# Queries stored once and split head by head, and two turning steps moved in their pipelines

## The reference

```python
h = layernorm(x) * (1 + ca) + sa
x = x + ga * attn(h, Wq, Wk, Wv, Wo)       # 16 heads, 4 key/value heads of 64, rotary, ALiBi, softmax over 1024 keys
h = layernorm(x) * (1 + cb) + sb
x = x + gb * ffn(h, ...)                   # two layers of local attention and gated MLP
...
# in attn
q = (x @ Wq).reshape(b, l, H, HD); k, v with KV = 4 heads, repeated 4 times
attn = softmax(rope(q) @ rope(k).T / sqrt(HD) + slopes * rel)
# in each of the 2 layers of ffn: 8 heads of 64, window 64 (this window and the one before it)
q, k = l2norm(q) * qs, l2norm(k) * ksc, both rotated and scaled by position
x = x + softmax(8 * q @ k.T + mask) @ v @ wo
x = x + (a * gelu(g)) @ w2 + b2
```

## Time and profile before

| | |
|---|---|
| median of 3 runs | 1131.87 us (1130.56 to 1132.34) |
| profiled execution, own time | 1133.57 us |
| its span, first to last instruction | 1131.8 us |
| TensorE busy | 1062.1 us (94%) |
| VectorE busy | 833.3 us (74%) |
| GpSimd busy | 747.3 us (66%) |
| ScalarE busy | 670.9 us (59%) |
| first matmul of the global attention | at 107.50 us |

### The profile page before, as it was taken

How to read it: one execution, slowest core, us unless ns; L and a number is a source line. 1 busy time by engine, 2 the same in 40 slices (tenths; PEclk the granted TensorE clock), 3 DMA queues, 4 the chain that set the end, 5 groups by cost and what they waited for, 6 DMA issues and landing times. The chain is left out here.

```text
span 1131.8 us, 23099 instructions
## 1 busy us (share of the span) xinstructions
PE 1062.1 (94%) x8304; PEld 654.9 (58%) x8304; DVE 833.3 (74%) x1522; ACT 670.9 (59%) x1222; POOL 747.3 (66%) x510
## 2 busy tenths in 40 slices
PE   6884799999999999999999999889999797999988
PEld 3552455555555555555555554766677694776778
DVE  6995666666666666666666674589999689999857
ACT  2552366566665665666666655047887556887744
POOL 3662466767686767776676768679986238756526
PEclk9996799999999999999999999999999999999989
DMA  8899622524315124242152100101111100111101
GB/s 255 276 275 357 161 57 48 112 53 93 80 50 122 40 66 104 67 92 69 48 113 71 44 20 21 38 10 32 33 43 34 25 2 19 33 34 33 44 17 36
DMA packets 82624, 88.48 MB, mean 78 GB/s; under 512 B 32036, under 2 KB 65360, under 8 KB 82512
## 3 DMA queue, kind: packets, MB, share of 16 engines
q1 hardware_dynamic: 82512, 87.01, 29.9%
HBM read 53.04 MB, written 24.24 MB: 68 GB/s over the span
## 5 line engine op out<-in xcount | busy, mean ns | idle before, releaser
L871 DVE CUSTOM_DVE_ANT_0 junk<-psum,alibi 128x1024 bf16<-128x1024 f32 x256 | 313.2, 1223 | 200.7 <-PE psum L942 191.8
L843 ACT ACTIVATE E<-psum,keybias_sb 128x1024 f32<-128x1024 f32 x256 | 274.7, 1112 | 229.6 <-PE psum L966 216.3
L774 POOL TENSOR_TENSOR sum_p<-sum_p,E 128x1024 f32<-128x1024 f32 x96 | 232.4, 2421 | 90.4 <-ACT E L843 85.8
L978 PE MATMUL psum<-E,V 128*64 128x512 f32 x1024 | 248.1, 605 | 0.0
L942 PE MATMUL psum<-KH,QH 64*128 64x512 f32 x512 | 118.7, 459 | 12.9 <-PEq L274 7.4
L978 PEld LDWEIGHTS psum<-E,V 128*64 128x64 f32 x1024 | 62.2, 136 | 112.3 <-issue 98.4
L780 POOL TENSOR_TENSOR sum_p<-sum_p,xpos_sb 128x1024 f32<-128x1024 f32 x32 | 76.3, 2384 | 69.0 <-DVE xpos_sb L881 69.0
L942 PEld LDWEIGHTS psum<-KH,QH 64*128 64x128 f32 x512 | 49.5, 189 | 121.9 <-DVE M L871 84.5
L966 PE MATMUL psum<-QH,KH 64*128 64x512 f32 x512 | 102.2, 395 | 2.1 <-DVE M L871 2.1
L966 PE MATMUL psum<-QL,KH 64*128 64x512 f32 x512 | 101.6, 392 | 0.0
L966 PE MATMUL psum<-QH,KL 64*128 64x512 f32 x512 | 101.5, 392 | 0.0
(11 more groups left out here) (149 smaller groups left out, 2008.3 us busy)
## 6 DMA issues: line engine op xcount, KB each, us to landing
QH<-qa_scratch SPq DMA_DIRECT2D x64, 256.0 KB, 4.2
qa_scratch<-tH SPq DMA_DIRECT2D x8, 1024.0 KB, 5.4
qa_scratch<-tL SPq DMA_DIRECT2D x8, 1024.0 KB, 7.9
QL<-qa_scratch SPq DMA_DIRECT2D x64, 128.0 KB, 4.2
vp_att<-v_att SPq DMA_DIRECT2D x64, 128.0 KB, 2.3
XF<-inverse_scratch SPq DMA_DIRECT2D x30, 256.0 KB, 3.4
KH<-k_scratch SPq DMA_DIRECT2D x16, 256.0 KB, 3.9
KL<-k_scratch SPq DMA_DIRECT2D x16, 256.0 KB, 5.1
```

Of the source, the lines that this page charges most:

```text
L774: pool.tensor_tensor(sum_p[:, s, :], first, E[:, k % 4, :], ALU.add)\
L843: act.activation(E[:, k % 4, :], scores(k % 2), ACT.Exp, bias=kb).then_inc(exp_done, 1)
L871: dve.tensor_tensor_reduce(junk[:, :], banks(max_bank(i, k), 2), alibi[:, s, :], -1.0, BIG, ALU.add, ALU.min, M[:, s, k:k + 1]).then_inc(m ...
L978: last = pe.matmul(banks(6 + i % 2)[HD * ch:HD * ch + HD, :], V[:, g, k, :], E[:, k % 4, ch * 512:(ch + 1) * 512], start=(k == 0), stop=(k ...
```

## The change

- The queries are stored once, in float32 as turned and scaled (`tQ`), not as a high and a low part; only keys keep both. The query low parts in `low_parts` go. `load_qa` has three transfers: the lower 64 partitions get the head as it is, the upper ones its two halves exchanged, which is why the products for the maxima take their blocks there in another order.
- In each head the split is made on the spot: ScalarE rounds 512 columns into `QL` (`high_q`), GpSimd subtracts that from the float32 values (`low_q`), ScalarE rounds all 1024 columns in place (`round_q`). For head 0 it is done at the end of the first stage, for heads 1 and 2 at the start of the second, for the others three heads ahead. SyncE issues the query loads ahead of those of a key group.
- In the first stage the turning, the high and low parts, the stores and the loads of head 0 have lag 4 in place of 3.
- In the local attention `turn_e` and `take_eT` stand last in their lists with lag SCORES, that is at the end of the step that makes the exponentials, no longer early in the next one. `multiply_v` stands second, and `weighted` ahead of `square_sums`.

```diff
-    qa_d = nc.dram_tensor("qa_scratch", (B, PAIRS, 2, P, TB, P), F32, kind="Internal").ap()
+    qa_d = nc.dram_tensor("qa_scratch", (B, PAIRS, P, TB, P), F32, kind="Internal").ap()
...
         def load_qa(sp, i, s):
-            high, low = parts_of(qa_d, i // H, i % H)
-            for ch in range(2):
-                rows, half = slice(HD * ch, HD * ch + HD), slice(TB // 2 * ch, TB // 2 * (ch + 1))
-                sp.dma_start(QH[rows, s, :].bitcast(F32).rearrange("p (t c) -> p t c", c=P), high)\
-                    .then_inc(ld_qa[s], 16)
-                sp.dma_start(QL[rows, s, :].bitcast(F32).rearrange("p (t c) -> p t c", c=P), low[:, half])\
+            a = HD * (i % H % 2)
+            q = qa_d[i // H, i % H // 2, a:a + HD]
+            sp.dma_start(raw(s)[0:HD].rearrange("p (t c) -> p t c", c=P), q).then_inc(ld_qa[s], 16)
+            for n in range(2):
+                half = slice(TB // 2 * (1 - n), TB // 2 * (2 - n))
+                sp.dma_start(raw(s)[HD:P, 512 * n:512 * n + 512].rearrange("p (t c) -> p t c", c=P), q[:, half])\
                     .then_inc(ld_qa[s], 16)
...
-                        for n, (done, tensor) in enumerate(((high_done, tH), (low_done, tL))):
-                            need(sp, done, NPT * (t + 1))
-                            for d, blocks in ((qa_d, slice(0, H // 2)), (k_d, slice(H // 2, NBLK))):
-                                sp.dma_start(d[b, :, n, :, tiles, :].rearrange("j p t c -> p j (t c)"),
-                                             tensor[:, pair % PS, blocks, :].bitcast(F32)).then_inc(t_out[b][pair % PS], 16)
-
-                    over_tiles([(first_heads, 3), (store_pair, 3), (store_v, 2)])
+                        need(sp, high_done, NPT * (t + 1))
+                        sp.dma_start(qa_d[b, :, :, tiles, :].rearrange("j p t c -> p j (t c)"), tQ[:, pair % PS])\
+                            .then_inc(t_out[b][pair % PS], 16)
+                        need(sp, low_done, t + 1)
+                        for n, tensor in enumerate((tH, tL)):
+                            sp.dma_start(k_d[b, :, n, :, tiles, :].rearrange("j p t c -> p j (t c)"),
+                                         tensor[:, pair % PS].bitcast(F32)).then_inc(t_out[b][pair % PS], 16)
+
+                    over_tiles([(first_heads, 4), (store_pair, 4), (store_v, 2)])
...
+                    pool.wait_ge(qh_done, 1)
+                    pool.tensor_tensor(QL[:, 0, :], raw(3)[:, 0:512], raw(0)[:, 0:512], ALU.subtract).then_inc(ql_done, 1)
...
+                    act.wait_ge(ld_qa[3], 16 * Q_LOADS)
+                    act.activation(QH[:, 0, :], raw(3), ACT.Copy).then_inc(qh_done, 1)
...
-                        for n in range(NPT):
-                            need(dve, high_done, NPT * t + n + 1)
-                            dve.scalar_tensor_tensor(part(tL, t // 2 % PS, n, t), turned_part(n),
-                                                     HD ** -0.5 if n < NPT - 1 else 1.0,
-                                                     part(tH, t // 2 % PS, n, t).bitcast(F32), ALU.mult, ALU.subtract)\
-                                .then_inc(low_done, 1)
+                        need(dve, high_done, NPT * (t + 1))
+                        dve.tensor_tensor(k_part(tL, t // 2 % PS, t), turned_part(NPT - 1),
+                                          k_part(tH, t // 2 % PS, t).bitcast(F32), ALU.subtract).then_inc(low_done, 1)
...
-                    over_tiles([(products, 2), (low_parts, 3), (stats_ahead, 1)])
+                    over_tiles([(products, 2), (low_parts, 4), (stats_ahead, 1)])
...
-                    over_tiles([(x_transposed, 1), (project, 2), (transposed, 3)])
+                    over_tiles([(x_transposed, 1), (project, 2), (transposed, 4)])
...
+                    def low_q(i, s):
+
+                        need(pool, ql_high, i)
+                        pool.tensor_tensor(QL[:, s, :], raw(s)[:, 0:512], QL[:, s, :].bitcast(F32), ALU.subtract)\
+                            .then_inc(ql_done, 1)
...
+                            if n == 3 and i + 3 < HEADS:
+                                low_q(i + 3, (i + 3) % 4)
...
+                    for i in range(1, 3):
+                        low_q(i, i)
...
+                    def high_q(i, s):
+
+                        need(act, ld_qa[s], raw_landed(i))
+                        act.activation(QL[:, s, :], raw(s)[:, 0:512], ACT.Copy).then_inc(ql_high, 1)
+
+                    def round_q(i, s):
+
+                        need(act, ql_done, i + 1)
+                        act.activation(QH[:, s, :], raw(s), ACT.Copy).then_inc(qh_done, 1)
...
+                            if k == 4 and i + 3 < HEADS:
+                                high_q(i + 3, (i + 3) % 4)
                             if k == 5 and i + 3 < HEADS:
                                 alibi_row(i + 3, (i + 3) % 2)
+                            if k == 1 and i >= 1 and i + 2 < HEADS:
+                                round_q(i + 2, (i + 2) % 4)
...
+                    for i in range(1, 3):
+                        high_q(i, i)
+                        round_q(i, i)
                     alibi_row(2, 0)
                     take_m(0, 0)
...
-        return [(square, NORMS), (take_eT, PV), (exponentials, SCORES), (take_v, SCORES), (take_qkT, TURN_QK),
-                (take_oT, PV), (take_hT, TURN_X)]
+        return [(square, NORMS), (exponentials, SCORES), (take_v, SCORES), (take_qkT, TURN_QK),
+                (take_oT, PV), (take_hT, TURN_X), (take_eT, SCORES)]
...
-        return [(maxima, SCORES), (normalise, TURN_QK), (square_sums, NORMS), (weighted, PV), (products, PROJECT),
+        return [(maxima, SCORES), (normalise, TURN_QK), (weighted, PV), (square_sums, NORMS), (products, PROJECT),
                 (residual, OUT), (denominators, SCORES)]
...
-        return [(multiply_qk, SCORES), (turn_e, PV), (project_v, SCORES), (multiply_v, PV),
-                (project_qk, PROJECT), (turn_qk, TURN_QK), (turn_o, PV), (project_out, OUT), (turn_x, TURN_X)]
+        return [(multiply_qk, SCORES), (multiply_v, PV), (project_v, SCORES), (project_qk, PROJECT),
+                (turn_qk, TURN_QK), (turn_o, PV), (project_out, OUT), (turn_x, TURN_X), (turn_e, SCORES)]
```

More of the change, by code:

```diff
@@ L175, in adaln_block @@
             sb = sb_in(ph)
-            NBLK, VS, PS = (H + KV) // 2, 4, 3
+            VS, PS = 4, 3
             v_sb = sb("v_sb", [P, VS, KW])
-            tH = sb("tH", [P, PS, NBLK, 2 * P], F32R)
-            tL = sb("tL", [P, PS, NBLK, 2 * P], F32R)
+            tQ = sb("tQ", [P, PS, H // 2, 2 * P])
+            tH = sb("tH", [P, PS, KV // 2, 2 * P], F32R)
+            tL = sb("tL", [P, PS, KV // 2, 2 * P], F32R)
             w_sb = sb("w_sb", [P, QW + 2 * KW])
@@ L246, in need_pair_sent @@
                 if pair >= 0:
-                    eng.wait_ge(t_out[pair // (TB // 2)][pair % PS], 64 * pairs_in(pair // (TB // 2), pair))
+                    eng.wait_ge(t_out[pair // (TB // 2)][pair % PS], 48 * pairs_in(pair // (TB // 2), pair))
             def need_landed(eng, b):
                 for last in range((b + 1) * TB // 2 - PS, (b + 1) * TB // 2):
-                    eng.wait_ge(t_out[b][last % PS], 64 * pairs_in(b, last))
+                    eng.wait_ge(t_out[b][last % PS], 48 * pairs_in(b, last))
                 for s in range(VS):
@@ L262, in adaln_block, with q_part, k_part @@
             LN_BATCHES = ((0, 2), (2, TB), (TB, T))
-            def part(tensor, s, n, t):
+            def q_part(s, n, t):
                 a, b = PARTS[n]
-                return tensor[:, s, a // 2:b // 2, t % 2 * P:t % 2 * P + P]
+                return tQ[:, s, a // 2:b // 2, t % 2 * P:t % 2 * P + P]
+            def k_part(tensor, s, t):
+                return tensor[:, s, :, t % 2 * P:t % 2 * P + P]
             def turned_part(n):
@@ L532, in transposed @@
                         for n, (a, b) in enumerate(PARTS):
-                            need(pe, low_done, NPT * (t - 1) + n + 1)
+                            if n < NPT - 1:
+                                need(pe, high_done, NPT * (t - 1) + n + 1)
+                            else:
+                                need(pe, low_done, t)
                             for j in range((b - a) // 2):
@@ L733, in head @@
                         need(sp, qk_done, TB * i)
+                        if i + 3 < HEADS:
+                            if i + 3 == H:
+                                need_landed(sp, 1)
+                            load_qa(sp, i + 3, (i + 3) % 4)
                         if i % GROUP == 0 and i // GROUP + 1 < HEADS // GROUP:
@@ L932, in max_step @@
                         if k == 0:
-                            need(pe, ld_qa[s], 64 * (i // 4 + 1))
+                            need(pe, qh_done, i + 1)
                             if i % GROUP == 0:
@@ L941, in max_step @@
                             rows = slice(HD * ch, HD * ch + HD)
```

(7 more changed lines are left out.)

19 lines of the change are left out of this document (12 added, 7 removed).

## The result

The changed kernel takes 1105.81 us (median of 4 runs, 1104.65 to 1109.63) beside 1132.11 for the kernel before: a ratio of 0.9774, with a 95% interval from 0.9756 to 0.9792. That is 26.3 us faster. The forecast was 14.3 us, and its range ended at 1109: the sign was right, the size was not, and nearly a third of the gain lies in a stage for which none was forecast. The profiled execution spans 1102.8 us (own time 1104.65), 29.0 less than that of before. The profiled one of before was the slowest of its four and this one the fastest of its four: 1.5 and 1.2 us of the 29.0 are that choice. Single traces differ by more than their second digit: in four traces with this same first stage (this one, the changed kernel again, all but the local lists, the exchanged local list) the heads' first matmul starts at 87.10, 86.05, 86.54 and 87.70.

The account below looks back on a forecast made before the run. VectorE was taken to bound the first stage, stores close behind, and TensorE the heads and local attention. First stage -16.5, entry to heads +2.2, heads 0, local attention 0 gave -14.3: 1117.5 us, range 1109 to 1127.

Parts of the forecast that it names:

- The local attention: Local attention: same instructions in another order, steps of 8.7 us stay full; bounds -5 and +6, taken as 0.
- What bounds the first stage: First stage: VectorE busy 56.5 of 57.0 us sets the pace, stores close behind with DMA at 0.89 share.
- a constant (6.1 us, 4.6 for three): End of first stage: last low part to heads' first matmul, 6.1 us with four SyncE stores, 4.6 with three.
- The stage's terms: First stage: the terms that put the heads' start at 91, a gain of 16.5 us, between 12 and 19.
- The pace 3.83: First stage: TensorE becomes the next limit and runs gapless at 3.83 us per tile, against 4.94 before.
- The store queue's 1.6: End of first stage: delay from stores and head-0 loads queued close to the end; bounds nothing or 5.5, taken as 1.6.
- rival B: First stage: stores bind it, 0.9 of today's pace in its second half, gain only 8, time 1126; chance 0.14.
- Entering the heads: Start of the heads: the query split behind the landed loads costs +2.2 us, between nothing and 5.
- Head 1 is 2 us late: Start of the heads: copy, subtraction, copy and handovers (3.04 plus 0.3) after landing, loads 1.3 us sooner.
- margin 0.13: Each head: VectorE's running sum slips 0.15 us behind GpSimd's subtraction, against 0.28 of slack, so hidden by 0.13.
- rival D: Heads: GpSimd's subtraction beyond 1.40 us costs TensorE one for one; slower from 1.86 us, example 1151; chance 0.07.
- the drain: Local attention, end of each layer: scores now stand behind the turning, costing about 1 us each.

Follow-up runs that it names:

- all but the local lists: The changed kernel with the local attention's three lists (TensorE, ScalarE, VectorE) of the kernel before; 1110.65 us, ratio 0.9813.
- the exchanged local list: The changed kernel with the value projection put back between the scores and `multiply_v` in TensorE's local list; 1109.73 us, ratio 0.982.
- lag alone: The kernel before with only the first stage's lags moved from 3 to 4, queries still stored twice; 1130.96 us, ratio 0.9991.

## Why the prediction was off, step by step

- **The place of the gain, right in the main.** The first stage pays, the heads neither gain nor lose. The local attention pays too, which the forecast left out, and that is the largest miss: of the 14.7 us that the traces gave beyond the forecast, 3.9 lie in the first stage, 2.1 in the entry to the heads and 8.6 in the local attention.
- **What bounds the first stage, wrong in one point.** "VectorE sets the pace there, with the stores close behind" holds for the pace, not for the end. The stores behind the last low part were put down as a constant (6.1 us, 4.6 for three), as if the queue were empty ahead of them. The lag alone shows that it was full: four us won on VectorE left the heads where they were. In the changed kernel's first trace the term fits by luck: 4.9 us from the last low part to the first matmul, and 2.7 in its second trace.
- **The stage's terms.** Forecast heads at 91, measured 87.10. The pace 3.83 was 3.73 (1.2 us in 12 tiles): TensorE's 2.25 + 0.43 + 1.15 overlap a little. The start of tile 3 was 28.64, not 29.5 (0.9). From tile 15's products to the last low part 8.9, not 9.3 (0.4): the forecast had the last turnings at the half clock, and here they ran at the full one; in the second trace they took 2.40 us at the half clock, as in before, and the part 9.7. The store queue's 1.6 did not come: rival B's wait was there, 4.12 us on ScalarE and 2.27 on TensorE, but taking it away gained nothing. Sum 20.4 in place of 16.5.
- **Entering the heads, wrong: +2.2 forecast, 0.1 measured.** The step that failed is "Head 1 is 2 us late", as if that delayed the first scores. It was also less late than forecast, 0.4 us by the start of its maxima (9.80 behind the heads' first matmul, before 9.36): its loads landed 2.6 us sooner and not 1.3. The timeline of after, with the landing, the split of head 1, its first maximum, the row of maxima and the first scores:

```profile
93.78 0.63 ACT L846 ACTIVATE QL<-QH 128x512 fp32r<-128x512 f32 x1 [3.42 <-DMA QH<-qa_scratch]
...
96.90 1.66 PE L995 MATMUL psum<-KH,QH 64*128 64x512 f32 x4 [1.09 <-ACT QH L851]
...
100.75 0.25 ACT L869 ACTIVATE mrow<-psum 8x128 fp32r<-8x128 f32 x1
...
102.01 1.22 DVE L923 CUSTOM_DVE_ANT_0 junk<-psum,alibi 128x1024 bf16<-128x1024 f32 x1
...
103.53 0.80 PE L1019 MATMUL psum<-QH,KH 64*128 64x512 f32 x2 [2.19 <-DMA QM<-mrow]
```

  The scores need eleven maxima, and VectorE makes one every 1.38 us from 88.23 on without a stop (the eleventh starts at 102.01), because in this lead three PSUM slots let TensorE run ahead: head 1's matmul at 96.90 let TensorE wait 1.1 us and VectorE not at all. The other chain (landing, two splits, alibi, row of maxima, its transfer) ends 0.3 us behind the eleventh maximum, where before the scores followed that maximum by 0.15. So the split lay hidden with next to nothing to spare: with 0.61 us more on GpSimd for each split and a landing 8.1 us behind the heads' first matmul in place of 6.7, the scores came 2.6 us later.
- **The heads, right.** Subtraction 1.27 forecast, 1.29 measured; running sum 1.4, measured 1.40; margin 0.13, measured 0.07 to 0.11 (417.92 plus the full 1.27 is 419.19, not 419.15, and gives 0.09); cost 0, measured 0.1 us in 580. The price of rival D is right too: one for one past the margin. Of the Trainium skill's rule (SBUF — State Buffer, Who interferes with whom), by which the two exclude one another for a whole instruction, the runs here leave 0.13 us of overlap at the end, after 0.14 in the earlier trace rows.
- **The local attention, wrong: 0 forecast, 8.6 in the traces, 4.8 to 6.3 in the medians.** "One change of array shape fewer may give 0.1 a step" was seen and then set off against fills and drains at "about 1 each". The step gave 0.14 (8.73 to 8.59), and within a layer that was given back, in part as forecast: the second tile's scores of the first layer are 19.4 us sooner where the first tile's are 20.4. The term that failed is the drain, the passage behind a layer's last scores. It was put down as a loss of about 1 each and gained in both layers: some 1.8 between the layers and some 2 at the end are the order's. And before lost 1.2 and 3.5 us more there to half clock, which no step of the sum had looked at. Why the passages gain more than the turning that moved ahead of the last scores (about 1.0 each) stays open.

Sum of the corrected terms: -20.4 + 0.1 + 0.1 - 0.2 - 3.0 - 5.6 = -29.0, in two traces; the medians have 26.3. What stays open is why the clock falls in one drain and not in the other.

## What to carry over

Where a stage ends in a queue of stores, follow that queue back from the end of the stage, and ask whether it ever runs dry; only then is the work of the engines what ends it. Where two resources are near full, price an edit against the next bound, and expect two edits to give more together than apart. An engine that is held up in a lead phase costs nothing until the count of slots ahead of the true bound (here the maxima on VectorE) is used up; count them before you add a delay.

## What the runs showed of the hardware

- The issue of one transfer on SyncE doesn't always take the same time. Stores took 0.37 us in the changed kernel at 78.68, after SyncE had paused for 1.6 us, and 1.19 to 1.57 at 82 to 86, one behind the other; the DMA engines were at their full share both times. The longest took 5.07 (lag alone, `k_scratch<-tL` at 77.93). What stands behind it in SyncE's list waits.
- TensorE's clock fell to half at the first stage's end in every trace. In the changed kernel TensorE stood idle from 81.1 to 87.1, and the clock was 0.98 in 80 to 84 us and 0.50 in 84 to 104. In 16 to 24 us it fell in seven traces (mean there 0.57 to 0.79) and stayed full in the others. The executions of the changed kernel go from 1102.8 us of span at a mean clock of 0.987 to 1107.8 at 0.979.
- Two 512-wide projections took 0.97 us behind one change of array shape and 1.05 between two.
- A VectorE sum of two SBUF operands (1.22 us alone) that began while GpSimd's subtraction ran ended 1.09 us behind the subtraction's end, twice: it waited for all but the last 0.13.
